# One block DMA per token, its source row picked by a register, in place of an index computation, eight gathers and eight block copies

## The reference

```python
w = weights[conditions]                              # conditions: 32 numbers below 200, weights (200, 32, 32)
y = einsum('bct,bcd->bdt', x, w)                     # x: (32, 32, 256)
xt = y.reshape(1024, 256)                            # 1024 tokens of width 256
probs = softmax(xt @ w_router)                       # 16 experts
top_w, top_i = top_k(probs, 4); top_w /= sum(top_w)
g = silu(xt @ we1[e]) * (xt @ we3[e])                # per expert, hidden 128
moe = sum over the 4 chosen e of top_w * (g @ we2[e])
shared = silu(xt @ ws1) * (xt @ ws3) @ ws2           # hidden 512
out = x + shared / 5 + moe * 4 / 5
```

## Time and profile before

| | |
|---|---|
| median of three runs | 194.9 us (193.61, 194.9, 198.0) |
| span of the profiled execution | 213.9 us |
| PE busy | 143.7 us, 67% of the span |
| POOL busy | 112.2 us, 52% |
| DVE busy | 106.9 us, 50% |
| ACT busy | 80.2 us, 37% |
| mean clock granted to PE | 0.870 of full speed |

### The profile page before, as it was taken

One profiled execution on the slowest core, in us unless ns is written; L12 is line 12 of the kernel. 1 busy time (PEld: TensorE's weight loads), 2 busy tenths in 40 slices (PEclk: granted clock), 3 DMA queues, 4 the chain that ended last, 5 costly groups with the idle time before them and its releaser, 6 DMA issues.

```text
span 213.9 us, 3234 instructions
## 1 busy us (share of the span) xinstructions
PE 143.7 (67%) x859; PEld 120.6 (56%) x860; DVE 106.9 (50%) x271; ACT 80.2 (37%) x169; POOL 112.2 (52%) x117
## 2 busy tenths in 40 slices
PE   7923599689999349549969688888869878410000
PEld 3322567479878243139959586878769877300000
DVE  3536738789995166014444343443533444205870
ACT  2202159253475231022654453735546464500000
POOL 4779970187887787400444455463643737350050
PEclk9997589999999967976988999999988999965555
DMA  4953422045479822264443434434424311119960
GB/s 132 321 138 94 130 77 75 0 136 178 155 223 294 277 98 97 76 160 137 116 133 92 135 98 125 116 106 121 124 78 130 116 50 52 50 46 320 377 259 25
DMA packets 28508, 29.23 MB, mean 137 GB/s; under 512 B 4295, under 2 KB 25422, under 8 KB 28497
## 3 DMA queue, kind: packets, MB, share of 16 engines
q1 hardware_dynamic: 23168, 19.60, 31.6%
q0 software_dynamic: 4048, 8.57, 11.2%
q10 hardware_dynamic: 1280, 0.93, 1.3%
HBM read 19.61 MB, written 11.44 MB: 145 GB/s over the span
## 4 chain that ended last, share of the span: by engine, by line
PE 31%; POOL 21%; DMA 11%; DVE 11%; issue 10%; another core or an unknown queue 7%; ACT 5%; SPq 2%; POOLq 0%; ACTq 0%; DVEq 0%
POOL sent L440 17%; PE up_ps L905 12%; PE down_ps L916 6%; PE down_ps L895 6%; DMA w_lo<-result 5%; PE gate_ps L886 3%; POOL cond_g L411 3%; DVE cond_bd L569 3%; ACT y_hi L523 2%; DVE g L763 2%; DMA itok_all<-in_itok_B 2%; DMA cond_g<-in_L_cond_weights,gather_idx 2%; ACT sil L527 1%; SPq L386 1%
## 5 line engine op out<-in xcount | busy, mean ns | idle before, releaser
L451 POOL DMA_INDIRECT result<-yo,dest_i x47 | 46.3, 986 | 55.7 <-ACT yo L535 44.5
L440 POOL DMA_INDIRECT sent<-rows,slot_i x32 | 36.4, 1137 | 19.9 <-DVE slot_i L668 10.5
L905 PE MATMUL up_ps<-w_hi,y_hi 128*128 x94 | 30.2, 321 | 0.0
L905 PE MATMUL up_ps<-w_lo,y_hi 128*128 x94 | 27.9, 297 | 0.0
L905 PE MATMUL up_ps<-w_hi,y_lo 128*128 x94 | 27.9, 296 | 0.0
L746 DVE TENSOR_TENSOR g_lo<-down_ps,g_hi 128x256 fp32r<-128x256 f32 (+1 forms) x24 | 10.1, 419 | 34.3 <-ACT g_hi L519 18.8
L535 ACT ACTIVATE yo<-down_ps,row_w 128x256 f32<-128x256 f32 x47 | 19.8, 472 | 12.2 <-PE down_ps L916 8.3
L751 DVE TENSOR_TENSOR y_lo<-gate_ps,y_hi 128x512 fp32r<-128x512 f32 (+1 forms) x24 | 16.3, 680 | 13.1 <-ACT y_hi L523 11.7
L886 PE MATMUL gate_ps<-ident,xt 128*128 128x128 f32 x94 | 15.7, 293 | 5.6 <-DMA xt<-sent 5.6
L905 PEld LDWEIGHTS up_ps<-w_hi,y_hi 128*128 128x128 f32 x94 | 19.3, 205 | 0.1
L905 PEld LDWEIGHTS up_ps<-w_hi,y_lo 128*128 128x128 f32 x94 | 19.2, 204 | 0.0
(11 more groups left out here) (152 smaller groups left out, 324.4 us busy)
## 6 DMA issues: line engine op xcount, KB each, us to landing
xt<-sent SPq DMA_DIRECT2D x48, 129.0 KB
w_raw<-in_L_ffn_we SPq DMA_DIRECT2D x48, 128.0 KB
w_lo<-result SPq DMA_DIRECT2D x8, 512.0 KB, 7.5
w_raw<-in_L_ffn_ws SPq DMA_DIRECT2D x12, 128.0 KB
acc<-in_x SPq DMA_DIRECT2D x2, 512.0 KB, 4.8
out<-acc ACTq DMA_DIRECT2D x7, 128.0 KB, 4.4
result<-yo,dest_i POOLq DMA_INDIRECT x47
sent<-rows,slot_i POOLq DMA_INDIRECT x32
```

The costliest lines, as they stand in the source:

```text
L440: pool.indirect_dma_start(sent, bass.IndirectOffsetOnAxis(ap=slot_i[:, t, k:k + 1], axis=0), y_row[:, k % 2, t, :], None,).then_inc(token_ ...
L451: pool.indirect_dma_start(result, bass.IndirectOffsetOnAxis(ap=dest_i[:, n, i:i + 1], axis=0), yo[:, r, i, :], None, bounds_check=RESULTS ...
L905: last = pe.matmul(gu_ps[b][:, i, :], tx[a][:, b, i, k * P:(k + 1) * P], of(w, experts[i], k * 2 * H, (k + 1) * 2 * H), start=(m == 0), st ...
```

## The change

The condition numbers are no longer broadcast into SBUF. SP and ACT each read 8 of them per half into registers, from the tensor in DRAM, and issue for each one DMA of 32 rows by 128 bytes from `cond_w` straight into its block on the diagonal of `cond_bd`, which DVE now zeroes first of all. Of each half's 16 items SP takes the first 8 and ACT the other 8. PE waits for all 16 DMAs of a half (`bd_in`) where it waited for four copies. The `iota`, the index arithmetic, the gathers and the block copies are gone, and so are four SBUF tensors. SP issues its 16 blocks ahead of the shared weights, ACT its 16 ahead of its first activation.

```diff
--- before.py
+++ after.py
@@ -64,7 +64,7 @@
     RING = 4
     LAG = 2
     assert POOL_E + sum(ROUNDED) == E and POOL_E + sum(AMID) + sum(BEHIND) + LAST == E
-    assert KEY & (KEY - 1) == 0 and NSH == RAW and E % RAW == 0 and H == P and D == 2 * H and HALF == 512 and TH == 4
+    assert KEY & (KEY - 1) == 0 and C * C == T and NSH == RAW and E % RAW == 0 and H == P and D == 2 * H and HALF == 512 and TH == 4
 
     with ExitStack() as ctx:
         def sb(name, shape, dt=F32):
@@ -77,11 +77,6 @@
         result = nc.dram_tensor("result", [RESULTS, D], F32).ap()
 
         acc = sb("acc", [P, TT, D])
-        itok_all = sb("itok_all", [P, B], I32)
-        chan = sb("chan", [P, Q])
-        chan_i = sb("chan_i", [P, Q], I32)
-        gather_idx = sb("gather_idx", [P, TT], I32)
-        cond_g = sb("cond_g", [P, TT, C])
         cond_bd = sb("cond_bd", [P, TT, P])
         y_hi = sb("y_hi", [P, KD, T], F32R)
         y_lo = sb("y_lo", [P, KD, T], F32R)
@@ -171,14 +166,10 @@
         t_sil, t_gated = (v[:, :, 0:2 * P].rearrange("p b (i d) -> p b i d", i=2) for v in (sil, g))
 
         x_in = [sem(f"x_in{h}") for h in range(2)]
-        itok_in = sem("itok_in")
         wr_in = sem("wr_in")
-        iota_done = sem("iota_done")
         const_done = sem("const_done")
-        idx_done = sem("idx_done")
-        gathered = [sem(f"gathered{h}") for h in range(2)]
         zeroed = sem("zeroed")
-        bd_done = sem("bd_done")
+        bd_in = [sem(f"bd_in{h}") for h in range(2)]
         warm_ready = sem("warm_ready")
         cond_done = sem("cond_done")
         y_hi_done = sem("y_hi_done")
@@ -236,7 +227,7 @@
 
         x_tiles = x.rearrange("(g q) c t -> (q c) g t", q=Q)
         out_tiles = out.rearrange("(g q) c t -> (q c) g t", q=Q)
-        cond_rows = cond_w.rearrange("s c d -> (s c) d")
+        itok_row = itok.rearrange("(a b) -> a b", a=1)
 
         def w_slot(u):
 
@@ -309,11 +300,24 @@
             eng.wait_ge(combined[t], 3)
             eng.dma_start(out_tiles[:, t, :], acc[:, t, :]).then_inc(out_done, 16)
 
+        def blocks_of(eng, part):
+
+            for h in range(2):
+                first = TH * Q * h + part * TH * Q // 2
+                registers = [eng.alloc_register(f"cond{part}_{h}_{i}") for i in range(TH * Q // 2)]
+                eng.load(registers, itok_row[0:1, first:first + TH * Q // 2])
+                for i, register in enumerate(registers):
+                    t, q = divmod(first + i, Q)
+                    r = slice(q * C, (q + 1) * C)
+                    s = eng.snap(register, donate=True, min_val=0, max_val=cond_w.shape[0] - 1)
+                    if h == 0 and i == 0:
+                        eng.wait_ge(zeroed, 1)
+                    eng.dma_start(cond_bd[r, t, r], cond_w[bass.ds(s, 1)].rearrange("s c d -> (s c) d")).then_inc(bd_in[h], 16)
+
         block = ctx.enter_context(nc.Block())
 
         @block.sync
         def _(sp):
-            sp.dma_start(itok_all[:, :], itok.rearrange("(a b) -> a b", a=1).to_broadcast((P, B))).then_inc(itok_in, 16)
             for h in range(2):
                 sp.dma_start(acc[:, TH * h:TH * h + TH, :], x_tiles[:, TH * h:TH * h + TH, :]).then_inc(x_in[h], 16)
 
@@ -329,9 +333,15 @@
                           .rearrange("e p k h -> (e p) k h") for w in (we1, we3))
                 load(k, s1, s3, we2[bass.ds(e, 1)].rearrange("e h d -> (e h) d"))
 
-            for k in range(NSH):
+            def load_shared(k):
                 s1, s3 = (w.rearrange("(k p) (s h) -> s p k h", p=P, h=H)[k] for w in (ws1, ws3))
                 load(k, s1, s3, ws2[k * H:(k + 1) * H, :])
+
+            blocks_of(sp, 0)
+            load_shared(0)
+            load_shared(1)
+            load_shared(2)
+            load_shared(3)
 
             for k in range(RAW):
                 if k < LEAD:
@@ -389,8 +399,6 @@
 
         @block.gpsimd
         def _(pool):
-            pool.iota(chan_i[:, :], pattern=[[-C, Q]], base=0, channel_multiplier=1).then_inc(iota_done, 1)
-
             pool.iota(iota_i[:, :], pattern=[[1, E]], base=0, channel_multiplier=0).then_inc(const_done, 1)
             pool.iota(item_i[:, :], pattern=[[1, ITEMS_UP]], base=0, channel_multiplier=0).then_inc(const_done, 1)
             pool.iota(where_i[:, :, :], pattern=[[TOP_K * P, TT], [1, TOP_K]], base=0, channel_multiplier=TOP_K).then_inc(const_done, 1)
@@ -406,14 +414,6 @@
             pool.affine_select(out=tri_e[:, :, :], in_=tri_e[:, :, :], compare_op=ALU.is_gt, fill=0.0, base=0,
                                pattern=[[1, E], [-1, E]], channel_multiplier=0).then_inc(const_done, 1)
 
-            pool.wait_ge(idx_done, Q)
-            for t in range(TT):
-                pool.indirect_dma_start(
-                    cond_g[:, t, :], None, cond_rows,
-                    bass.IndirectOffsetOnAxis(ap=gather_idx[:, t:t + 1], axis=0),
-                ).then_inc(gathered[t // TH], 16)
-
-
             pool.wait_ge(zeroed, 2)
             for n in range(NSH - LEAD + POOL_E):
 
@@ -460,6 +460,7 @@
         @block.scalar
         def _(act):
             act.dma_start(wr[:, :, :], w_router.rearrange("(k p) e -> p k e", p=P)).then_inc(wr_in, 16)
+            blocks_of(act, 1)
             act.wait_ge(wr_in, 16)
             act.activation(wr_pair[:, :, 0, :], wr[:, :, :], ACT.Copy).then_inc(wr_hi_done, 1)
 
@@ -545,37 +546,20 @@
 
         @block.vector
         def _(dve):
+            dve.memset(cond_bd[:, :, :], 0.0).then_inc(zeroed, 1)
             dve.memset(warm, 0.0).then_inc(warm_ready, 1)
-            dve.wait_ge(iota_done, 1)
-            dve.tensor_copy(chan[:, :], chan_i[:, :]).then_inc(route, 1)
-            dve.wait_ge(route, 1)
-            dve.wait_ge(itok_in, 16)
-            for q in range(Q):
-                r = slice(q * C, (q + 1) * C)
-                dve.tensor_scalar(gather_idx[r, :], itok_all[r, q::Q], float(C), chan[r, q:q + 1], ALU.mult, ALU.add).then_inc(idx_done, 1)
-            dve.memset(cond_bd[:, :, :], 0.0).then_inc(zeroed, 1)
             dve.memset(zeros, 0.0).then_inc(zeroed, 1)
             dve.memset(item_e_i[:, :, :], 0).then_inc(zeroed, 1)
             dve.wait_ge(wr_hi_done, 1)
             dve.tensor_tensor(wr_pair[:, :, 1, :], wr[:, :, :], wr_pair[:, :, 0, :].bitcast(F32), ALU.subtract).then_inc(wr_lo_done, 1)
             dve.wait_ge(zeroed, 3)
 
-            def block_diagonal(h):
-
-                dve.wait_ge(gathered[h], 16 * TH)
-                for q in range(Q):
-                    r = slice(q * C, (q + 1) * C)
-                    t = slice(TH * h, TH * h + TH)
-                    dve.tensor_copy(cond_bd[r, t, r], cond_g[r, t, :]).then_inc(bd_done, 1)
-
             def rest_of_lead(k):
                 dve.wait_ge(lead_hi, k + 1)
                 dve.tensor_tensor(w_lo[:, w_slot(k), :], w_raw[:, k, :], w_hi[:, w_slot(k), :].bitcast(F32), ALU.subtract).then_inc(lead_split, 1)
 
             rest_of_lead(0)
-            block_diagonal(0)
             rest_of_lead(1)
-            block_diagonal(1)
             for h in range(2):
                 for k in range(KD):
                     dve.wait_ge(y_hi_done, KD * h + k + 1)
@@ -592,7 +576,7 @@
                 dve.tensor_tensor(g[:, h, :], sil[:, h, :], up_ps[h][:, :], ALU.mult).then_inc(g_done, 1)
 
 
-            done = [1]
+            done = [0]
 
             def step(ins):
                 done[0] += 1
@@ -778,7 +762,7 @@
             for h in range(2):
 
                 pe.wait_ge(x_in[h], 16)
-                pe.wait_ge(bd_done, Q * (h + 1))
+                pe.wait_ge(bd_in[h], 16 * Q * TH)
                 for k in range(KD):
                     for t in range(TH * h, TH * h + TH):
                         c = (t % TH) * P
```

## The result

The kernel became slower, by a little: median 197.6 us (196.57 to 197.78, four runs) against 194.9 beside it, a ratio of 1.012 with a 95% interval of 1.007 to 1.017. Forecast were 193.2 us. The time lies inside the range and within 2%, but on the other side of no change. The profiled execution has a span of 195.7 us. Its first send is at 43.46, where the one of before had 41.43. Here and in the table further down the medians are over all runs, while the ratios leave out the slow runs of each kernel (over 1.5% above its fastest), so a ratio need not be the quotient of the two medians beside it.

What follows compares the result with a forecast made beforehand. The start of POOL's first send (41.43 us) bounds the kernel. Blocks win 7.0 us, but later weights and POOL's splits holding the routing chain leave 41.4 - 39.7 = 1.7: 194.9 becomes 193.2 us, range 187.8 to 197.8.

Steps and rivals of the forecast that it cites:

- A half is 2.0 + 8 x 0.42 = 5.4 us.: SP and ACT queues: register loads of 2.0 us plus eight block DMAs at 0.42 us make a half 5.4 us.
- break-even of 6.2 us: Head of SP and ACT queues: a half costing more than 6.2 us makes the first send later than before.
- rival three: Head of SP and ACT queues: dearer loads and issues delay weights and send, 198.0 to 199.3 us; chance 0.22.
- The landing: DMAs from DRAM: blocks and weights land 2.2 us after issue, raw buffer 2 at 19.6.
- the wait changes its owner: ACT's `y_hi`: the wait on the copies is replaced by one on the late weights; last `y_lo` 7.0 us earlier.
- the hold of the port: DVE's routing chain: operations with two SBUF inputs wait for POOL's running split, 4.5 us in all.
- Rival one: DVE's routing chain: the port doesn't hold it; first send at 34.6, 6.8 us gained, 188.1 us; chance 0.22.
- The 0.6 us by which DVE was to lengthen the splits: POOL's splits: DVE operations slipping in between move their end by 0.6 us, from 34.3 to 34.9.
- POOL's end: End of POOL's splits, forecast at 34.9 us; `top_w` on DVE was to come out practically there, at 34.2.
- The 1.3 us of one round trip: Register loads from HBM: by the skill a half's two loads are 2.6 us instead of 2.0, giving 194.4.

Runs made afterwards that it cites:

- fixed_rows: Changed kernel without the register reads, block b taken from fixed row b of `cond_w`; 210.44 us beside 215.36 for the kernel before, ratio 0.977.
- no_read_splits: Changed kernel with POOL's eight split operations turned into memsets that read nothing from SBUF; 190.69 us, ratio 0.977 of the kernel before.
- late_lead: Changed kernel with roundings and rests of the first two shared weights moved behind the four `y_hi` and `y_lo`; 195.85 us, ratio 1.003 of the kernel before.
- before_thirds: Kernel before, with only POOL's split operations cut into thirds; 192.25 us, ratio 0.990 of the kernel before; its profiled execution took 203.8 us.
- hybrid_two: Kernel before, second half's blocks by 8 DMAs on ACT and 8 on SP behind its shared weights, POOL's splits in thirds; 190.06 us, ratio 0.981.
- weights_first: Changed kernel with the 12 shared weight loads ahead of SP's 16 blocks instead of behind; 194.14 us, ratio 0.995 of the kernel before.
- hybrid: Kernel before, first half by gathers and copies, second by 16 block DMAs on ACT from one read; 210.33 us beside 215.36, ratio 0.976.

## Why the prediction was right or wrong

**The step that failed: "A half is 2.0 + 8 x 0.42 = 5.4 us."** It was 3.63 us of loads for the first and 1.76 for the second, with 4.1 for each half's blocks, 6.8 on the mean ((15.46 - 1.8) / 2). By its own break-even of 6.2 us that is rival three. Each half 0.6 over it, twice, puts the first send at 42.6; measured are 42.85 and 43.46. Both factors were low. The loads were 5.4 us in place of 4.0: the eight numbers were cheap (0.97 and 0.91 us), the first address load was dear (2.66 us, while x was in flight; 0.85 later on). The blocks were 0.51 each in place of 0.42: a block's parts were summed, but the queue does not take the next one at once.

**The landing.** Raw buffer 2 was issued in full at 19.95, and POOL started on it at 23.11, 3.2 us later where 2.2 was taken. With 3.0 us from the queue's head and 0.4 back from faster weight issues (1.5 us a buffer instead of 1.63), this is about the 3.5 by which POOL's first split missed 19.6. Its last ended at 38.45, 3.55 behind the forecast. From POOL's first split to the first send the forecast had 20.1 us (19.6 to 39.7) and the runs 20.35, so nearly all of the 3.8 us by which the send missed 39.7 was there when POOL started.

**Right: the wait changes its owner.** PE had the second half's blocks at 17.15, `y_hi` was released by the weights' rounding, and `fixed_rows` shows that the queue's head, POOL's first split and the send move together.

**Right in sum, not in its places: the hold of the port.** 4.5 us were forecast; the four operations of the chain were held for 4.1 us in one execution and 4.6 in the other. `lg` and `prob` cost 0.6 each beyond their own time, `pick` was not held (0.69), `top_f` in its place was (1.3), and `top_w` cost 1.6. Rival one is out. Two casts, `iota_e` and `item`, took 1.8 us each; the prediction had not seen them. They lay beside the logits and cost little: in `no_read_splits` DVE, done with them early, waited 2.48 us for PE. Nor had it seen that PE would run at its lower clock level then: the stretch from the last `y_lo` to `lg`, carried over from the kernel before (2.57 us), took 3.85 and 3.07. That this did no more harm was luck, since a later `lg` was held for less. The 0.6 us by which DVE was to lengthen the splits were right (15.34 us instead of 14.7).

**Right, but no rule: POOL's end.** `top_w` did come out at the end of the splits (38.51 and 38.45), but by timing: in `late_lead` it was through two operations sooner.

The Trainium skill ("SBUF — State Buffer", section "Who interferes with whom") has the rule behind three of the four stops, an operation with two SBUF inputs blocked for a whole POOL operation that reads SBUF: `top_w` at 1.79 us beside splits of 1.8, and `lg` at 0.29 beside POOL's fills, which read nothing, agree. The order of turns in `before_thirds`, 15.75 us for four copies, is more than one operation's wait. The 1.3 us of one round trip (the Trainium skill, "Runtime: NRT & Kernel Launch", section "The ~15µs preamble/postamble breakdown") gave 2.6 us for a half's loads; the mean of the two halves is 2.7 (3.63 and 1.76), so by it the forecast would have been 194.4, nearer but still short of the result.

## What to carry to other kernels

Small DMAs on a queue are paid by what stands behind them. Before moving loads to a queue, sum register loads and issues by their start to start distance, compare with the break-even of the first late item behind them, and put them where the queue idles (`hybrid_two`). When a stage becomes earlier, look at what it now runs beside: here 3.7 us won by the blocks were given back, 4.1 us to POOL's reads of SBUF and 1.5 to PE. Where one engine is held by another's operations, look first at when the other starts: the first send followed POOL's first split, whatever was won on PE in between.

## What the runs showed of the hardware

- Loads of 8 numbers from DRAM into registers took 0.88 to 1.33 us on SP and of 16 took 1.88 to 1.93; on ACT 0.90 to 1.46, and 2.45 to 2.56 for 16. With x and the weights in flight ACT's took 3.16 (`weights_first`) and 4.30 (`hybrid_two`) for 8 and 5.62 for 16. In front of each comes a load of the tensor's address, 0.83 to 0.99 us where little was in flight, 1.33 on SP behind the weights in `weights_first`, 2.0 to 3.1 while x was. That the traffic makes the difference is read from these places and not tested by itself.
- A block DMA addressed by a register came every 0.51 us on SP (0.48 on ACT in `hybrid`), one with a fixed address every 0.46.
- Beside POOL operations that read SBUF, DVE's casts (0.18 us became 1.8) and copies (four in 5.72 us, 1.16 elsewhere) are held too, not only operations with two SBUF inputs. Beside POOL's fills, which only write, two casts and a `tensor_tensor` were not (0.20, 0.18 and 0.29 us).
- Since each stop ends with a POOL operation, the chain on DVE moved in step with POOL: 20.34 to 20.35 us from POOL's first split to the first send in four executions.
- With thirds on POOL back to back, four small copies once took 15.75 us.
